# Attention, then experts, on one core: key-tile maxima sent as single columns, row-tiled projections, one key tile's exponentials added by DMA

## The reference, cut to what matters

```python
xn = layernorm(x)                                  # x: (8, 1024, 256)
h  = layernorm(xn) * ln_scale + ln_bias
c_q, c_kv = h @ w_down_q.T, h @ w_down_kv.T        # 128 wide
q, k, v = heads(c_q @ w_up_q.T), heads(c_kv @ w_up_k.T), heads(c_kv @ w_up_v.T)   # 16 heads of 64
q, k = rope(q), rope(k)
attn = softmax(q @ k.T / 8)
s = (attn @ v) @ w_out.T + xn
g = silu(moe(xn) + xn)                             # top 2 of 8 experts, capacity 2561
out = x + s * g
```

## Time and profile before

| | |
|---|---|
| median of 3 runs (lowest to highest) | 3657.75 us (3653.6 to 3657.8) |
| the profiled execution: its time, its span | 3655.32 us, 3653.8 us |
| mean granted TensorE clock | 0.998 of full speed |
| PE, DVE, ACT, POOL busy, of the span | 99%, 87%, 76%, 33% |
| attention, first to last pair | about 240 to 2600 us |

### The profile page before, as it was taken

The page is one execution under the profiler, slowest core; times in us unless marked ns, Lnnn a source line. Parts: engine busy times, 40 slices in busy tenths (PEclk is TensorE's granted clock), DMA queues, the critical chain, the costliest instruction groups (busy, mean ns, idle before and its releaser), DMA issues. The chain is left out here.

```text
span 3653.8 us, 77190 instructions
## 1 busy us (share of the span) xinstructions
PE 3599.4 (99%) x24217; PEld 2364.0 (65%) x24217; DVE 3195.1 (87%) x4341; ACT 2759.1 (76%) x4016; POOL 1199.8 (33%) x1178
## 2 busy tenths in 40 slices
PE   7999999999999999999999999999999999999999
PEld 5754554545544554545554555454699999999999
DVE  8889999999999999999999999999777777777799
ACT  5778888888878888888888888888766666666665
POOL 2212222222222222222222222232366666666400
PEclk9999999999999999999999999999999999999999
DMA  7985767676666666666667676765666666666798
GB/s 257 358 283 142 185 156 186 157 185 161 180 160 176 170 174 169 171 171 166 177 165 181 160 186 156 184 162 136 193 222 215 217 223 216 214 224 216 235 369 274
DMA packets 378436, 724.74 MB, mean 198 GB/s; under 512 B 105277, under 2 KB 253886, under 8 KB 342272
## 3 DMA queue, kind: packets, MB, share of 16 engines
q0 software_dynamic: 83504, 340.66, 36.2%
q1 hardware_dynamic: 294864, 383.23, 31.8%
HBM read 453.60 MB, written 138.81 MB: 162 GB/s over the span
## 5 line engine op out<-in xcount | busy, mean ns | idle before, releaser
L1180 ACT ACTIVATE at_ex<-at_st 128x1024 f32<-128x1024 f32 x1024 | 1048.8, 1025 | 138.3 <-PE at_st L1327 132.8
L1383 PE MATMUL at_pv<-at_ex,at_v 128*64 128x512 f32 x4096 | 991.6, 605 | 0.0
L1037 DVE TENSOR_REDUCE at_mx<-at_fr 128x1 fp32r<-128x512 f32 x1024 | 705.9, 689 | 202.5 <-PE at_fr L1393 169.6
L1204 ACT ACTIVATE at_fr<-at_fr 128x512 f32<-128x512 f32 x1024 | 603.4, 589 | 243.0 <-PE at_fr L1393 229.7
L1383 PEld LDWEIGHTS at_pv<-at_ex,at_v 128*64 128x64 f32 x4096 | 248.3, 136 | 471.1 <-issue 462.2
L1050 DVE TENSOR_TENSOR at_sum<-at_sum,at_ex 128x1024 f32<-128x1024 f32 x448 | 545.3, 1217 | 3.7 <-ACT at_ex L1180 3.4
L1393 PE MATMUL at_fr<-at_kfar,at_qh 64*128 64x512 f32 x1024 | 459.7, 449 | 5.9 <-DVE at_mx L1037 4.5
L1390 PE MATMUL at_fr<-at_kdif,at_qh 64*128 64x512 f32 x1024 | 461.4, 451 | 1.8 <-DVE at_mx L1037 0.9
L1327 PE MATMUL at_st<-at_qh,at_kh 64*128 64x512 f32 x2048 | 452.8, 392 | 3.8 <-DMA at_top<-at_mneg 3.7
L1390 PEld LDWEIGHTS at_fr<-at_kdif,at_qh 64*128 64x128 f32 x1024 | 187.7, 183 | 413.7 <-issue 356.9
L1327 PE MATMUL at_st<-at_ql,at_kh 64*128 64x512 f32 x2048 | 452.0, 391 | 0.0
(11 more groups left out here) (213 smaller groups left out, 6359.4 us busy)
## 6 DMA issues: line engine op xcount, KB each, us to landing
at_cq<-scr_c SPq DMA_DIRECT2D x62, 1024.0 KB, 6.1
at_ck<-scr_c SPq DMA_DIRECT2D x62, 1024.0 KB, 5.2
at_sum<-at_sum POOLq DMA_DIRECT2D x95, 512.0 KB, 6.0
scr_v<-pj_v SPq DMA_DIRECT2D x64, 512.0 KB, 6.8
at_v<-scr_v SPq DMA_DIRECT2D x64, 512.0 KB, 6.6
mid_rec<-scr_rec SPq DMA_DIRECT2D x256, 128.0 KB, 5.1
scr_o<-mid_oT SPq DMA_DIRECT2D x64, 512.0 KB, 3.0
at_rotq<-at_swpq POOLq DMA_DIRECT2D x126, 256.0 KB, 4.6
```

The costliest lines, as they stand in the source:

```text
L1037: e.reduce_max(mx[k // QB][:, h * QB + k % QB:h * QB + k % QB + 1], fr[h][:, :], AX.X).then_inc(s_tr[h], 1)
L1180: e.activation(ex[k][:, :, :], st[u % 2][:, :, :], ACT.Exp, scale=SCALE).then_inc(s_exp, 1)
L1204: e.activation(fr[h][:, :], fr[h][:, :], ACT.Relu).then_inc(s_pos[h], 1)
L1383: mm = e.matmul(pv[n][rows[h], :], v[i.u][:, kt, rows[h]], ex[kt][:, h, :], start=(kt == 0), stop=(kt == KT - 1))
```

## The change

- **Maxima.** `turn_maxima`, `negate`, `mneg` and the identity operand go. SP sends each column of `mx` by a DMA of its own into 128 elements of a row of `top` (`max_row`, 16 per pair), placed in its queue where the maxima become ready. `one_row` holds -1 instead of 1, which takes over the sign.
- **Projections.** All four halves of a pair are split over the rows: k in groups 2 and 3, q in groups 6 and 7. `project` is left only ahead of the first pair. The copies on ACT, and `far_keys`, `high`, `out_copy`, move to fit; on DVE `turn_cos`, `turn_sin` of k and `low` of q.
- **Broadcasts.** The reciprocals are written at the end of a turn (`gather`) and read back in the next turn (`each`), a half behind the second and a half behind the fifth of the columns.
- **Sums.** The exponentials of key tile 3 (`SENT`) are added to `sums[n][0]` by an accumulating DMA of POOL (`add_sent`) instead of DVE; in the last pair DVE does it (`add_kept`). `ex[3]` is written again only when that DMA has landed.

```diff
-        NADD = KT - 2
-        ADDED = (1, 1, 2, 3, 4, 4, 5, 6)
+        NADD = KT - 3
+        SENT = KT // 2 - 1
+        ADDED = (1, 1, 2, None, 3, 3, 4, 5)
...
-            def max_rows(j, n):
-                e.wait_ge(s_neg, j.n(2, n + 1))
-                for h in range(2):
-                    r = rows[h].start
-                    e.dma_start(top[j.u][r:r + 1, bank[n]].bitcast(F32).rearrange("o (t q) -> o t q", q=P),
-                                mneg[n][h * QB:(h + 1) * QB, :].bitcast(F32)).then_inc(s_mrow[n], 16)
+            def max_row(j, k, h):
+
+                wait_apart(e, s_tr[h], j.n(NSLOT_Q, k + 1), s_apart_s)
+                r, col = rows[h].start, h * QB + k % QB
+                e.dma_start(top[j.u][r:r + 1, k * P:(k + 1) * P].bitcast(F32), mx[k // QB][:, col:col + 1].bitcast(F32),
+                            allow_slow_non_contiguous=True).then_inc(s_mrow[k // QB], 16)
...
-            def broadcast(i, halves, k=0):
+            def gather(i, halves, k=0):
                 e.wait_ge(s_recc, i.n(1, k + 1))
                 for n in halves:
                     e.dma_start(scr["rec"][i.n(), n:4:2, :].rearrange("h (p k) -> p h k", p=P), recc[:, :, n, :]).then_inc(s_recd, 16)
+
+            def each(i, n):
+
+                e.wait_ge(s_recd, i.n(32, 32))
+                for h in range(2):
+                    e.dma_start(rec[n][rows[h], :], scr["rec"][i.n(), 2 * h + n, :].unsqueeze(0).broadcast_to((DH, HALF))).then_inc(s_rec[n], 16)
+
+            def broadcast(i, halves, k=0):
                 e.wait_ge(s_recd, i.n(32, 32 if k or len(halves) == 2 else 16))
                 for n in halves:
                     for h in range(2):
...
+                one = i.next(1)
+                older = prev and not (isinstance(i.n(), int) and i.n() < 2)
                 if ahead >= 3:
                     load(i.next(3), Q)
+                max_row(i, 5, 1)
+                max_row(i, 6, 0)
+                if older:
+                    each(prev.next(-1), 0)
+                max_row(i, 6, 1)
+                max_row(i, 7, 0)
+                max_row(i, 7, 1)
+                if older:
+                    each(prev.next(-1), 1)
                 if ahead:
-                    load_v(i.next(1))
-                max_rows(i, 1)
+                    load_v(one)
+                    max_row(one, 0, 0)
+                    max_row(one, 0, 1)
+                    max_row(one, 1, 0)
                 if ahead >= 3:
                     load(i.next(3), K)
+                if ahead:
+                    max_row(one, 1, 1)
+                    max_row(one, 2, 0)
                 if prev:
                     spread(prev, (0, 1))
                 if ahead:
-                    max_rows(i.next(1), 0)
+                    max_row(one, 2, 1)
+                    for k in (3, 4):
+                        for h in range(2):
+                            max_row(one, k, h)
+                    max_row(one, 5, 0)
                 if prev:
-                    if not (isinstance(i.n(), int) and i.n() < 2):
+                    if older:
                         store(prev.next(-1))
-                    broadcast(prev, (0, 1))
+                    gather(prev, (0, 1))
...
+            def add_sent(i, n):
+
+                e.wait_ge(s_exp, i.n(UNITS, KT * n + SENT + 1))
+                wait_apart(e, s_sum, i.n(2 * NADD, NADD * n + ADDED[SENT - 1]), s_apart)
+                e.dma_start(sums[n][0][i.u][:, :, :], ex[SENT][:, :, :], accum_op=ALU.add).then_inc(s_one[n], 16)
+
             def add_sums(i, n):
 
+                e.wait_ge(s_one[n], i.n(32, 16))
                 wait_apart(e, s_sum, i.n(2 * NADD, NADD * (n + 1)), s_apart)
                 e.dma_start(sums[n][0][i.u][:, :, :], sums[n][1][i.u][:, :, :], accum_op=ALU.add).then_inc(s_one[n], 16)
...
                 if prev:
                     add_sums(prev, 1)
+                if ahead:
+                    add_sent(i, 0)
                 if ahead >= 2:
                     add_swapped(i.next(2), Q)
                 if ahead:
                     add_sums(i, 0)
                 if ahead >= 2:
                     add_swapped(i.next(2), K)
+                if ahead:
+                    add_sent(i, 1)
...
+            def add_kept(i, n):
+
+                e.wait_ge(s_exp, i.n(UNITS, KT * n + SENT + 1))
+                e.wait_ge(s_sum, i.n(2 * NADD, NADD * n + ADDED[SENT - 1]))
+                acc = sums[n][0][i.u][:, :, :]
+                e.tensor_tensor(out=acc, in0=acc, in1=ex[SENT][:, :, :], op=ALU.add).then_inc(s_kept, 1)
+
...
-                due = [(j, u // KT, m) for m in (u % KT, u % KT + 1) if j and m % (KT // 2)]
-                return (due[:-1], due[-1:])
+                due = [(j, u // KT, m) for m in (u % KT, u % KT + 1) if j and m % (KT // 2) and m != SENT]
+                return (due, []) if u % KT + 1 == SENT else (due[:-1], due[-1:])
...
-                wait(e, s_sum, i.n(2 * NADD, NADD * (n - 1) + ADDED[k]))
+                if k == SENT:
+                    if n and isinstance(i.n(), int) and i.n() == NPAIR - 1:
+                        e.wait_ge(s_kept, 1)
+                    else:
+                        wait(e, s_one[1 - n], i.n(32, 16) if n else i.n(32, -16))
+                else:
+                    wait(e, s_sum, i.n(2 * NADD, NADD * (n - 1) + ADDED[k]))
                 e.activation(ex[k][:, :, :], st[u % 2][:, :, :], ACT.Exp, scale=SCALE).then_inc(s_exp, 1)
 
...
-                    if g == 1 and prev:
-                        out_copy(prev, 1)
                     if g == 1 and not prev:
                         rt["scalar"](e)
                     if g == 5 and not prev:
...
                         out_copy(i, 0)
                     if g < 2 or more:
                         gain(*slot_of(i, g), 0, s_x)
-                    if g == 0 and prev and ahead >= 2:
-                        proj_copy(two, Q, 1, pv[0])
-                    if g == 4 and ahead >= 2:
-                        proj_copy(two, K, 1, pv[1])
+                    if g == 1 and prev:
+                        out_copy(prev, 1)
+                    if g == 3 and more:
+                        high(one, K)
                     exps(i, 2 * g)
                     if g < 2 or more:
                         gain(*slot_of(i, g), 1, s_y)
+                    if g == 2 and ahead >= 2:
+                        proj_copy(two, K, 0, pv[1])
+                    if g == 6 and ahead >= 3:
+                        proj_copy(three, Q, 0, pv[0])
+                    if g == 7 and ahead >= 2:
+                        far_keys(two)
                     exps(i, 2 * g + 1)
                     if g == 4 and prev:
                         den_copy(prev, 1)
-                    if g == 1 and ahead >= 2:
-                        proj_copy(two, K, 0, pv[1])
-                    if g == 2:
-                        negate(i, 1)
-                    if g == 5 and ahead >= 3:
-                        proj_copy(three, Q, 0, pv[0])
-                    if g == 6 and more:
-                        negate(one, 0)
+                    if g == 3 and ahead >= 2:
+                        proj_copy(two, K, 1, pv[1])
+                    if g == 7 and ahead >= 3:
+                        proj_copy(three, Q, 1, pv[0])
                     if g == 0 and more:
                         high(one, Q)
-                    if g == 1 and more:
+                    if g == 1 and more and not prev:
                         far_keys(one)
-                    if g == 2 and more:
-                        high(one, K)
...
-            def project_row(j, x, k, h, dst):
+            def project_row(j, x, n, k, h, dst):
                 ws, cs = PASSES[k]
-                return e.matmul(dst[:, :], w[x][j.u][rows[h], ws, :], c[x][rows[h], cs, bank[1]],
+                return e.matmul(dst[:, :], w[x][j.u][rows[h], ws, :], c[x][rows[h], cs, bank[n]],
                                 start=(h + k == 0), stop=(ws == 1), skip_group_check=(h == 1))
 
-            def upper_rows(i, u, j, x, dst):
-
+            def upper_rows(i, u, j, x, n, dst):
+
+                if n == 0:
+                    e.wait_ge(s_ld[x][j.u], j.same(32, 32))
                 scores_free(i, u)
                 for k in range(3):
-                    mm = project_row(j, x, k, 0, dst)
+                    mm = project_row(j, x, n, k, 0, dst)
                     if k == 2:
                         mm.then_inc(s_upper, 1)
                     score(i, u, k, 1)
...
                         mm.then_inc(s_st, 1)
                     score(i, u + 1, k, 1)
 
-            def lower_rows(i, u, j, x, dst):
-
-                e.wait_ge(s_upper, i.n(2, 1 if x == K else 2))
+            def lower_rows(i, u, j, x, n, dst):
+
+                e.wait_ge(s_upper, i.n(4, n + (1 if x == K else 3)))
                 for k in range(3):
                     mm = score(i, u + 1, k, 0)
                     if k == 2:
                         mm.then_inc(s_st, 1)
```

(77 more changed lines are left out.)

34 lines of the change are left out of this document (16 added, 18 removed).

## The result

The changed kernel takes 3596.4 us (median of 4 runs, 3595.9 to 3597.3) against 3657.8 us before: ratio 0.9835, with a 95% interval of 0.9818 to 0.9852. The forecast was 3599 us, and 58 us were foretold where 61 came. Run again beside the experiments it took 3599.4 us against 3659.6, ratio 0.9841 (0.9824 to 0.9857).

What follows compares the result with a forecast made beforehand. PE's own instructions were taken to bound the kernel. Savings of 34.4 (projections), 19.7 (turning) and 4 us (waits) sum to 58, giving 3599 us; forecast range 3590 to 3612, 8-in-10 range 3588 to 3635.

Steps and rivals of the forecast that it cites:

- PE alone binds: Attention, 300 to 2600 us: PE is bound by its own instructions; other engines' work matters only where late for PE.
- Projections, 34 us: Groups 1, 2, 5, 6: 123 full half projections become split ones, each saving 0.28 us, 34.4 us in all.
- Turning, 20 us: Loop over pairs: dropping 127 matmuls that turn maxima, each holding PE 0.155 us, saves 19.7 us.
- Waits for `top`, 4 us: Scores waiting for rows of `top`: 3.7 us of PE waits go, counted as 4 with short ones.
- Column DMAs on SP: SP's queue: sixteen column DMAs replacing four add 7.5 us per pair, fitting in 19 us of waits; no cost.
- Landing in 4.0 us: Columns of `top` before the scores: each lands 4.0 us after issue, leaving a margin of 3.6 us.
- The sum by DMA: Key tile 3's exponentials: DVE loses 2 of 12 sums per pair, DMA share rises to 87%; gives nothing by itself.
- The broadcasts, nothing: Issued in groups 0 to 2, wanted in groups 4 and 7, the nearer some 15 us later; no effect.
- the rival of late rows: Columns land beyond their margin, so scores of units 0 and 8 wait: 3774 us at 9 us landing; chance 0.11.

Runs made afterwards that it cites:

- the 3793 us run: Changed kernel with the broadcasts read back at the end of the turn again, ahead of the next columns: 3793.4 us, ratio 1.0371 to the kernel before.

## Why the prediction was right, point by point

- **PE alone binds.** Right: 0.155 us on PE twice a pair, with nobody waiting for it, cost 20 us; 2.3 us of DVE work a pair cost nothing.
- **Projections, 34 us.** The mechanism was right, the term mis-sized: 25 us. I took the mean of 4.93 and 4.81 as the price of a full half. Full projections in the new order take 4.81 everywhere. The 0.12 us more of group 1 was, by the rows, PE waiting for a late gain, behind `out_copy` on ACT: the gain ends at 1212.35, the maxima's matmuls behind it start at 1212.40, and the projection 0.42 us later, where in group 5 it is 0.32:

```profile
1212.41 0.49 PE L1390 MATMUL at_fr<-at_kdif,at_qh 64*128 64x512 f32 x1
1212.83 0.50 PE L1429 MATMUL at_pv<-at_ck,at_wk 128*128 128x512 f32 x1
...
1231.75 0.39 PE L1390 MATMUL at_fr<-at_kdif,at_qh 64*128 64x512 f32 x1
1232.07 0.97 PE L1429 MATMUL at_pv<-at_cq,at_wq 128*128 128x512 f32 x3
```

The changed order of `out_copy` takes that away, 61 x 0.12 = 7 us; no run moves `out_copy` alone, so this cause is read and not tested. So the sum came out right for a reason that stood elsewhere: the price of a step was read where a wait was in it. That 9 us too much here and 12 us left out elsewhere nearly cancel is luck.

- **Turning, 20 us.** Right in size, by a group difference.
- **Waits for `top`, 4 us.** Nearly: by the group starts, group 4 had on average 5.45 us against 5.39 without waiting, 4 us over the pairs, and the 2.0 us of the last pair come on top. Groups 0 and 4 are besides 0.02 to 0.04 us shorter after, some 3 us, which I can't explain: with full projections they have their old length again, and groups 3 and 7 are 0.02 to 0.03 us shorter instead. 25 + 20 + 7 + 6 + 3 = 61.
- **Column DMAs on SP.** Wrong in size: 12.4 us more of SP a pair and not 7.5. The median issue (0.53 us) was even less than I took, but the ones behind others hold SP for up to 2.0 us. It fitted, so it cost nothing.
- **Landing in 4.0 us.** Wrong: 5.6 at the median and up to 7.3 in the 3793 us run, at a DMA share of 0.81. The columns were issued when the sum said, but the margin was about half as large.
- **The sum by DMA.** Right that it gives nothing; its landing was 5.9 us at the median, 6.0 assumed. What was missed is what it does to small transfers in SP's queue: with it they landed 3.4 us behind the load ahead of them, without it 1.3.
- **The broadcasts, nothing.** Wrong as a reason. It was right only in that the change makes them harmless: I asked when the broadcasts are wanted, and not what stands behind them in SP's queue. Without that line of the change the result would have been the rival of late rows, 3793 us. That this is near the 3774 worked out for it is luck: there both halves came 1.4 us late by a landing of 9 us, and here only half 1 came late, by 2.2 us, with a landing of 5.6 and an issue 4.4 us later, and a lower clock did the rest. Its chance of 0.11 rested on a margin that the order of SP's queue had made.

## What to carry to other kernels

Where one engine is busy throughout and nearly nothing waits, price a change by start-to-start differences of like stretches on that engine, and take the cleanest instance of each kind, not the mean. For every DMA that is moved in a queue, list what now stands behind it and how many bytes lie ahead of a small transfer with a deadline; an edit that looks like bookkeeping may be what makes the others possible. When a wait does appear, look at the granted clock behind it before its length is taken for the whole loss. A queue that issues DMAs has a busy time as well: count its waits before and after.

## What the runs showed of the hardware that was not expected

- A DMA of 128 elements of 4 bytes held SP for 0.47 us at the least, 0.53 at the median and up to 2.0 us behind others; eight more per pair cost SP 1.0 us each.
- Small transfers from SP, issued within 6 us behind a 1 MB load from SP, landed 4.3 to 7.3 us after their issue, by the start of the scores that waited for them, and never before the load (54 pairs, DMA share 0.81); moving the load behind them gave back 178 us over 64 pairs, by the ratios.
- Behind a wait of PE of 2.62 us in otherwise full work, the granted clock was 0.50 from 1201.3 to 1204.0 us of the 3793 us run, and matmuls started 0.43 us apart instead of 0.23. In that whole run PE was busy 71 us longer than in the changed kernel with the same work, out of 194 us lost.
- The small packets cost more than reckoned: q1's share rose from 33.6% to 40.4% in the same 600 us. In one pair that is 0.404 x 36.0 - 0.336 x 36.9 = 2.1 us of 16 engines, 17 ns for each of 2048 packets of 4 bytes, against the 7.9 ns of the 16-byte packets in the earlier trace rows. It is not the sum by DMA that makes them dear: without it the share is 40.6%. Nor is it a fixed price: the 1024 packets of eight more columns took 28 ns each, by 40.6% of 36.0 and 44.4% of 36.9 us from 300 to 2450 us.
